# A transformer-like layer with attention and eight experts: the first segment without attention, then experts, then the attention of all four batches

## The reference

```
xn  = layernorm(x)                        # x: 4 batches x 1024 tokens x 256
q   = xn @ Wq + bq + pe                   # 8 heads of 128
k,v = xn @ Wkv + bkv  (k + pe)            # one K and one V, shared by the heads
s   = softmax(causal(q @ k.T / sqrt(128))) @ v, heads joined, @ Wo
l   = xn @ router_w + router_b            # 8 experts; the best two of each token, softmax over the two
g   = silu(sum over the two of gate_e * (relu(xn @ w1[e] + b1[e]) @ w2[e] + b2[e]))   # 256 -> 1024 -> 256
out = x + s * g
```

## Time and profile before

| | us |
|---|---|
| median of 3 runs (lowest, highest) | 1190.79 (1185.71, 1192.36) |
| the profiled execution, own time | 1195.41 |
| its span, first to last instruction | 1193.6 |
| PE busy | 1060.6 (89%) |
| DVE busy | 865.0 (72%) |
| ACT busy | 575.4 (48%) |
| POOL busy | 512.4 (43%) |

### The profile page before, as it was taken

How to read it: one execution, slowest core, us unless ns; L and a number is a source line. 1 busy time by engine, 2 the same in 40 slices (tenths; PEclk the granted TensorE clock), 3 DMA queues, 4 the chain that set the end, 5 groups by cost and what they waited for, 6 DMA issues and landing times. The chain is left out here.

```text
span 1193.6 us, 28439 instructions
## 1 busy us (share of the span) xinstructions
PE 1060.6 (89%) x10323; PEld 842.4 (71%) x10323; DVE 865.0 (72%) x1545; ACT 575.4 (48%) x1310; POOL 512.4 (43%) x507
## 2 busy tenths in 40 slices
PE   5677867879999999999999978887999999999895
PEld 2355546668888888888888746565667767777684
DVE  6886688706766766754445578988989988999852
ACT  5498735513333333233333256656665655666631
POOL 3221022329998899940000015443444523454453
PEclk9798888999999999999999989999999999999997
DMA  8299745766666776672221239997899976999992
GB/s 288 58 205 197 168 98 120 153 166 160 170 173 174 197 185 172 161 172 53 68 68 49 76 68 176 170 177 150 155 161 173 166 142 129 154 153 172 164 207 71
DMA packets 435703, 176.65 MB, mean 148 GB/s; under 512 B 378218, under 2 KB 425780, under 8 KB 434932
## 3 DMA queue, kind: packets, MB, share of 16 engines
q1 hardware_dynamic: 371552, 133.22, 54.6%
q10 hardware_dynamic: 57204, 23.00, 8.2%
q0 software_dynamic: 6816, 18.62, 6.9%
HBM read 51.30 MB, written 31.46 MB: 69 GB/s over the span
## 5 line engine op out<-in xcount | busy, mean ns | idle before, releaser
L1664 POOL TENSOR_SCALAR b_ph<-b_pr,b_rrec 128x896 f16<-128x896 f32 (+4 forms) x120 | 112.7, 947 | 410.5 <-DVE b_rrec L1572 354.8
L1187 ACT ACTIVATE h<-psU,bias 128x256 f32<-128x256 f32 x312 | 129.3, 471 | 281.7 <-PE psU L1135 183.8
L1135 PE MATMUL psU<-bxT,w_p 128*128 128x256 f16 x1872 | 256.9, 275 | 4.8 <-issue 4.8
L1148 PE MATMUL psY<-w_p,hp 128*128 x1872 | 254.1, 273 | 0.0
L1208 DVE CAST hp<-h 128x512 f16<-128x512 f32 x156 | 88.3, 566 | 163.0 <-ACT h L1187 144.4
L1135 PEld LDWEIGHTS psU<-bxT,w_p 128*128 x1872 | 184.5, 99 | 27.6 <-issue 5.0
L1148 PEld LDWEIGHTS psY<-w_p,hp 128*128 128x128 f16 x1872 | 183.2, 98 | 21.2
L1455 ACT ACTIVATE b_pr<-b_psS,b_nmax 128x1024 f32<-128x1024 f32 (+1 forms) x192 | 140.4, 735 | 118.3 <-DVE b_nmax L1541 112.7
L1382 PE MATMUL b_psO<-b_pT,b_vp 128*128 128x128 f16 x2592 | 167.6, 222 | 29.9 <-DMA b_pT<-b_ph 19.0
L1382 PEld LDWEIGHTS b_psO<-b_pT,b_vp 128*128 128x128 f16 x2592 | 151.8, 99 | 42.8 <-issue 18.5
L1363 PE MATMUL b_psS<-b_kp,b_Q 128*128 128x512 f16 (+3 forms) x864 | 167.5, 331 | 0.1
(11 more groups left out here) (203 smaller groups left out, 1398.1 us busy)
## 6 DMA issues: line engine op xcount, KB each, us to landing
wstage<-in_L_ffn_w SPq DMA_DIRECT2D x64, 256.0 KB
expert_outputs<-y ACTq DMA_DIRECT2D x39, 256.0 KB
expert_rows<-rowx SPq DMA_DIRECT2D x74, 128.0 KB
...
```

The source lines that it names most:

```text
L1135: mm = eng.matmul(psU[w % U][:, g % 2, :].rearrange("p (t r) -> p t r", t=2), weight(n, a * W1 + c * H + g * P, P), bxT[n % 3][:, :, 2 * b ...
L1148: mm = eng.matmul(psY[n % 2][:, t, :], hp[n % 2][:, a, g, t * P:(t + 1) * P], weight(n, 2 * W1 + (2 * g + b) * D, D), start=(g == 0 and k ...
L1187: a = eng.activation(h32[w % 4][:, g, :], psU[w % U][:, g, :], ACT.Relu, bias=bias[:, ds(e * HT + 2 * q + g, 1)], scale=1.0 / WS)
L1664: a = eng.tensor_scalar(ph[k % 4][:, 2 * o:2 * o + w], pr[k % 3][:, o:o + w], rrec[:, at:at + 1], 1.0, ALU.mult, ALU.mult)
```

## The change

The segment `batch0` is replaced by `prologue`, which has no attention. It loads all of x (32 token tiles), normalises in pairs of tiles, turns them on the PE (`turn`), makes the logits, routes and lists the tokens. The high halves and the copies out of PSUM are split between ACT and DVE, the low halves between POOL and DVE, expert 0's weights between ACT and POOL. The turned rows of batch 0 stay in `xTb_next`; those of batches 1 to 3 are stored turned (`xT_d`). The splitting of Wq, Wo and Wkv (9 more pieces) goes to the end of POOL's list in the expert segment. `attention` has 32 heads instead of 24, in the order of batches 0 to 3. The last batch's 8 tiles are fetched and gated in heads 1 to 8 (`seq`), without `sr`, `added` or stores there, so the end of the kernel has no gating of them. The next batch's turned rows come in one plain DMA of 1 MB. At the end the head-7 part of two pairs' output projection stands before the last two `values`, and the last pair's addition is on DVE.

```diff
@@ attention @@
-    NH = 3 * HEADS
+    NH = 4 * HEADS
+    TILES = NT - QT
+    seq = list(range(TILES, NT)) + list(range(TILES))
+    turn_of = {c: s for s, c in enumerate(seq)}
@@ PE @@
-                    if i == 4 and n > QT:
+                    if i == 4 and n > HEADS:
                         eng.wait_ge(jl_, jobs.issued(k + 1))
-                        o_tile(n - 1)
+                        o_tile(n - HEADS - 1)
...
             rows_out(2, 0, HEADS - 1)
+            for s in (0, 1):
+                eng.wait_ge(al_, 4 * (NH - 1) + s + 1)
+                rows_out(PAIRS[s], HEADS - 1, HEADS)
             values(NH - 1, 2)
             values(NH - 1, 3)
             rows_out(1, 0, HEADS - 1)
-            for s in range(4):
+            for s in (2, 3):
@@ ACT and DVE, in the heads and at the end @@
-                        weigh(n - 1)
+                        weigh(seq[n - 1])
-            for c in range(NH - 1, NT):
-                weigh(c)
-                tanh(c)
-                if c % 2 == 0:
-                    o_high(NH - 1, c // 2 - NH // 2)
+            weigh(TILES - 1)
+            tanh(TILES - 1)
+            for s in range(4):
+                o_high(NH - 1, s)
...
-                if i == 0 and 2 <= n:
-                    o_gated(n - 2)
+                if i == 0 and n >= HEADS + 2:
+                    o_gated(n - HEADS - 2)
@@ SP @@
-                if m % 3 == 0 and m < 3 * QT and n + HEADS < NH:
+                if k % (5 * HEADS) == 2 and n + HEADS < NH:
...
-                    v["turned_rows"](eng, xTb[b % 2][:, m // 3], (b + 1) * QT + m // 3, xl[b % 2])
+                    eng.dma_start(xTb[b % 2][:, :, :, :].rearrange("p t h n -> p (t h n)"), xT_d[b - 1]).then_inc(xl[b % 2], 16)
@@ prologue (new), ACT @@
+            for k in range(2):
+                for p in range(k * TWOS // 2, (k + 1) * TWOS // 2):
+                    if p == k * TWOS // 2:
+                        eng.wait_ge(s_var, k + 1)
+                        eng.activation(rs[:, 0, sl], mv[:, sl, 1], ACT.Sqrt, bias=eps[:, :]).then_inc(s_sd, 1)
+                    high(p)
+                    if p >= 2 and p - 2 not in OUT_DVE:
+                        out(p - 2)
...
+                    if p >= 8:
+                        weights(p - 8)
@@ prologue, DVE @@
+            for g in range(4):
+                stats(g)
+            variance(HALF, slice(0, HALF))
+            stats(4)
+            rstd(1, slice(0, HALF))
+            for p in range(4):
+                normal(p)
+                after(p)
+            for g in (5, 6, 7):
+                stats(g)
...
+                normal(g - 1)
+                after(g - 1)
+            variance(NT, slice(HALF, NT))
+            normal(7)
+            after(7)
+            rstd(2, slice(HALF, NT))
+            for p in range(8, TWOS):
+                normal(p)
+                after(p)
...
+            choose(0)
+            choose(1)
+            blocks()
+            ranks()
+            slots(0)
+            for s in range(CHUNKS // 2):
+                one_hots(s)
+            slots(1)
+            for s in range(CHUNKS // 2, CHUNKS):
+                one_hots(s)
+            owners()
+            gates()
+            eng.wait_ge(s_sp, 1)
+            eng.tensor_scalar(who[:, :], psJ[:, 0:UNITS], float(T * 2), None, ALU.add).then_inc(v["who_"], 1)
@@ prologue, POOL @@
+            for p in range(TWOS):
+                if p not in BY_DVE:
+                    low(p)
+                if p >= 10:
+                    weights(p - 10)
...
+            for n in range(v["AHEAD"]):
+                v["gather"](eng, n)
```

1013 lines of the change are left out of this document (322 added, 691 removed).

## The result

| | before | changed |
|---|---|---|
| median, us | 1188.99 (4 runs) | 1175.97 (4 runs) |
| lowest, highest | 1185.71, 1192.36 | 1175.02, 1177.53 |
| profiled execution, own time and span | 1195.41, 1193.6 | 1175.02, 1173.2 |
| PE busy | 1060.6 (89%) | 1050.0 (90%) |

The ratio is 0.9892, with a 95% interval of 0.9858 to 0.9925: the change is faster by 1.1%. By the two profiled executions it is 20.4 us of span, by the medians 13.0.

A forecast was written before the change was run, and what follows sets the result against it. PE bounds the experts; the first segment and attention are chains across engines, with DMA nearly full. Terms -160.7 + 0 + 155.8 - 6 - 10 = -20.9 take the span from 1193.6 to 1172.7, median 1170, range 1158 to 1184.

The forecast's parts named there:

- The first segment: Everything before the experts: first expert matmul at 103.5 us, 160.7 earlier than before (bounds 150 and 170).
- DVE's first half: First segment, from 16.5: normalising, statistics, low halves, copies and variance on DVE take 13.8 us, to 30.3.
- ACT's second half: First segment, from 34.0: ACT's roundings, weight instructions and copies set the pace and take 19.5 us, to 53.5.
- DVE and POOL shutting each other out: Rival, first segment: POOL's subtractions and DVE's work block each other, +8 us, giving 1178; chance 0.15.
- The third rival: First segment: DMA backlog in SP's queue delays gathers, transposes and first expert blocks by some 12 us, giving 1182; chance 0.09.
- Experts: Expert segment: POOL's nine more weight pieces fit in free places and PE does not wait; 0 us (bounds -1, +4).
- Eight heads more: Attention segment: two added heads with K and V and six like heads 16 to 21 cost +155.8 us.
- Heads 0 to 8: First batch's heads in attention: less gating work and fewer SP transpose issues, less waiting behind 1 MB; -6 us.
- The two later loads: Attention, later batches' 1 MB loads of turned rows: nothing, as eight transposes and one load may cancel.
- The end: Last values and rows_out: no PE gaps without POOL's fetches, -7.5, and a shorter tail, -2.5; together -10 us (bounds -12, -2).
- The fourth rival: Attention: with DMA engines full, every output-tile head runs at 20.2 us, +31, giving 1201; chance 0.06.
- The last step, from span to median: Whole kernel: profiled execution of 1174.5 less the 4.6 us by which before's median lay below its profiled execution, giving 1170.

The follow-up runs named there:

- weights_late: Changed kernel with expert 0's sixteen ACT weight instructions and POOL's eight subtractions moved behind the last pair; median 1175.4 us, ratio to before 0.9816.
- turn_old: Changed kernel with the next batch's turned rows again by eight DMA transposes per batch instead of one 1 MB load; 1174.1 us, ratio to before 0.9804.
- gate_back: Changed kernel with gating-like work (DVE product, POOL addition, SP row loads and store) put back in heads 2 to 9 on spare buffers; one run, 1179.8 us.
- end_old: Changed kernel with the end's order undone: head 7's rows_out all behind the last two values, all four additions on POOL; one run, 1179.3 us.
- load_8: Changed kernel with the 1 MB load of turned rows cut into eight loads of 128 KB; 1167.5 us, ratio to before 0.9733.
- before_paced: Kernel before with the expert segment's 56 weight pieces spread over 70 places, so POOL issues at most two gathers in a row; 1198.8 us, ratio 1.0040.

## Why the prediction was right, and where it was not

**The first segment**: right to 0.5 us. 16.1 for 16.5, 34.4 for 34.0, ACT's last copy ending at 55.1 for 53.5, `who` at 85.7 for 84.5, first expert matmul at 103.0 for 103.5. ACT was the limit of the second half, as weights_late showed by moving its work away. Small errors cancelled: DVE's first half took 0.9 longer and ACT's second half 1.2 longer, the way from `who` 1.7 shorter. That the whole came out within 0.5 is in part luck.

**DVE and POOL shutting each other out** (the second rival, though the prediction once calls it the third) was real and far from its price of 8. It was not free: in the first half, where DVE has no idle time from 13.6 to 31.8, normalising took 0.8 longer beside POOL twice and a small operation of the variance another 0.8. That is 2.5, in a half that came out 0.9 longer than the sum. In the second half ACT stood for stretched normalising twice, 0.43 and 0.63, most of its 1.2. I was wrong on whom it touches. I took normalising as free of it, but four such operations took 3.52 beside POOL's subtractions, instead of 1.37:

```profile
39.03 1.37 DVE L552 TENSOR_SCALAR a_x_all<-a_x_all,a_mv,a_rs 128x256 f32<-128x256 f32 x4
...
44.93 3.52 DVE L552 TENSOR_SCALAR a_x_all<-a_x_all,a_mv,a_rs 128x256 f32<-128x256 f32 x4
```

```profile
44.50 1.16 POOL L696 TENSOR_TENSOR a_xp<-a_x_all,a_xp 128x512 f16<-128x512 f32 x1 [0.64 <-ACT a_xp L452]
45.61 2.37 POOL L704 TENSOR_TENSOR w_p<-a_w_raw,w_p 128x512 f16<-128x512 f32 x2
```

**The third rival**, SP's backlog, did not occur: the 3 MB of turned rows were issued by 58.3, and the transposes of gathered rows went out at 89.8, as soon as their rows were there.

**Experts**: 413.5, as before. The cover is thin: three kernels that start at 103 waited 0.2 to 1.0 for weights near 205, and the one that starts at 93 lost 5.0.

**Eight heads more**: 155.3 for 155.8, since their kinds were all on view in the trace before. **Heads 0 to 8**: -8.2 for -6. The size was near, its makeup was not: I put most of the possible gain on the eight transposes; turn_old shows that they cost nothing in most of these heads, and gate_back that the gating work was worth some 0.6 in nearly every head, 4.3 in all. The rest is two heads of before that waited for b_pT, which the prediction did not have, so the nearness of the size is luck.

**The two later loads**: the step that failed. "Nothing, where eight transposes and one load may cancel": heads 9 to 13 and 16 to 21 became 2.3 and 4.4 longer. 1 MB in front of a head's transposes cost heads 9 and 17 4.3 and 2.9 against eight loads, with the clock.

**The end**: -13.8 for -10. From the first of the last four `values` to its last matmul PE took 18.0 instead of 27.0: 9.0 where I took 7.5, since the `rows_out` behind the stutter had been slow too (66 in 8.54 at the granted clock of 0.86; end_old took 7.37 for them). The tail behind PE became 2.5 shorter, as taken, and end_old shows 2.3 of it in the small edits. The rest, 2.3, is that PE reached the last four `values` 27.1 after the last head's first maxima instead of 29.4, which the sum did not have. In before's profile it is one wait:

```profile
1131.66 2.67 PE L1382 MATMUL b_psO<-b_pT,b_vp 128*128 128x128 f16 x45 [2.51 <-DMA b_pT<-b_ph]
```

The three profiles of before wait 2.51, 0.60 and 1.83 at that place, and none of the changed kernel and its ten variants waits there. That the gating of the last eight tiles, which stood beside it, brings it about is likely; no run isolates it.

**The fourth rival**, slower heads throughout: heads 24 to 29 took 18.15 each. It did not happen.

So the sum of spans was -20.9 against -20.4, with errors of +6.7 (loads), -3.8 (end) and -2.2 (heads 0 to 8) that nearly cancel: the mechanisms of the large terms were right, the closeness of the sum is luck. **The last step, from span to median**, is the other one that failed. I subtracted 4.6, by which the profiled run of before lay above its median, from the changed kernel too. That offset belonged to one execution. The changed kernel's profiled run lay 0.9 below its median, load_8's 5.4 above, so the offset is not a constant that one kernel hands to the next. Without it the forecast would have been 1174.5, and 1176.0 was measured. Why the runs of before spread, from 1176.7 to 1203.2 over all chips, is not shown. PE's starvation, which moved from one row of gathers to another between its two profiles, is a candidate; before_paced, made to test it, was inconclusive, and load_8, whose four runs spread over 8.7, has no such row at its end.
